# Attention turn of a transformer block: far scores ahead of the last near values, gated transposes ahead of the near scores, low half of the normalised rows behind the near maxima

## What is computed

```
OFFSETS = sorted(set(range(0, 33)) | {48, 64, 96, 128, 192, 256, 384})
q, k, v = split(x @ Wqkv + bqkv)
scores[o] = q . shift(k, o) * scale + pos_bias[o]        # -inf where the offset leads before row 0
out = sum_o softmax(scores)[o] * shift(v, o)
gate = sigmoid(x @ Wgate + bgate)
x = layernorm(x + (out * gate) @ Wout + bout)
logits = relu(x @ rw1 + rb1) @ rw2 + rb2                 # top 2 of 8 experts, capacity 1024
x = layernorm(x + experts(x))
```

## Time and profile before

| | |
|---|---|
| median of 3 runs | 1965.34 us |
| lowest, highest | 1961.47, 1973.05 us |
| span of the profiled execution, first to last instruction | 1999.0 us |
| the profiled execution's own time outside its span | not given; the span alone is 1.7% above the median |
| mean granted TensorE clock in the profiled execution | 0.797 of 2.4 GHz |
| PE, DVE, ACT, POOL busy | 1512.8, 989.1, 905.2, 708.5 us |

### The profile page before, as it was taken

One profiled execution on the slowest core, in us unless ns is written; L12 is line 12 of the kernel. 1 busy time (PEld: TensorE's weight loads), 2 busy tenths in 40 slices (PEclk: granted clock), 3 DMA queues, 4 the chain that ended last, 5 costly groups with the idle time before them and its releaser, 6 DMA issues. The chain is left out here.

```text
span 1999.0 us, 72320 instructions
## 1 busy us (share of the span) xinstructions
PE 1512.8 (76%) x31232; PEld 1001.5 (50%) x31232; DVE 989.1 (49%) x2117; ACT 905.2 (45%) x1544; POOL 708.5 (35%) x654
## 2 busy tenths in 40 slices
PE   2447777887778787877778787887875499999970
PEld 1235554555554554545555555555643266776660
DVE  5214455454554455455545455554645355555525
ACT  3123353444435353435445353545443366656626
POOL 6022233433334253333334252433323113323335
PEclk9566786868777797878778787878766699999995
DMA  4483453535243443525242433525210424443328
GB/s 120 91 227 93 88 105 81 112 90 111 76 102 79 88 104 79 116 77 112 64 105 73 88 92 68 110 72 110 57 47 14 140 75 91 101 105 87 72 30 339
DMA packets 220103, 194.55 MB, mean 97 GB/s; under 512 B 66847, under 2 KB 207151, under 8 KB 219648
## 3 DMA queue, kind: packets, MB, share of 16 engines
q1 hardware_dynamic: 204464, 175.11, 35.3%
q0 software_dynamic: 15360, 15.10, 4.7%
HBM read 98.07 MB, written 86.18 MB: 92 GB/s over the span
## 5 line engine op out<-in xcount | busy, mean ns | idle before, releaser
L396 POOL TENSOR_TENSOR p<-p 128x512 f16<-128x512 f32 x96 | 129.0, 1344 | 440.5 <-ACT p L796 427.4
L810 ACT COPY featT<-gp 128x1024 f16<-128x1024 f16 x96 | 93.4, 1032 | 321.3 <-PE gp L541 321.3
L396 DVE TENSOR_TENSOR p<-p 128x512 f16<-128x512 f32 x96 | 94.7, 987 | 284.7 <-ACT p L796 282.8
L548 PE MATMUL gp<-featT,wr 128*128 128x512 f16 x768 | 209.4, 432 | 22.8 <-DVE mT L959 13.8
L1107 POOL DMA_INDIRECT disp<-y,sidx x128 | 174.1, 1360 | 53.6 <-issue 38.0
L1364 POOL DMA_INDIRECT xln<-y,place x64 | 104.9, 1639 | 216.0 <-DVE y L1506 175.7
L1402 PE MATMUL up<-rowsT,w 128*128 128x512 f16 x768 | 171.3, 383 | 9.6 <-DVE w L1479 6.1
L1416 PE MATMUL dn<-w,h 128*128 128x256 f16 x1536 | 170.1, 273 | 0.0
L623 PE MATMUL o<-v_near,p 128*32 128x66 f16 x2048 | 132.3, 203 | 40.0 <-issue 28.4
L795 ACT ACTIVATE p<-st 128x512 f16<-128x512 f32 x192 | 116.7, 608 | 101.0 <-PE st L592 98.1
L1416 PEld LDWEIGHTS dn<-w,h 128*128 128x128 f16 x1536 | 149.7, 98 | 17.3
(11 more groups left out here) (176 smaller groups left out, 3127.0 us busy)
## 6 DMA issues: line engine op xcount, KB each, us to landing
qk_dram<-qk SPq DMA_DIRECT2D x64, 256.0 KB, 2.5
v_near<-vs SPq DMA_DIRECT2D x224, 66.0 KB
qs<-qk_dram SPq DMA_DIRECT2D x96, 128.0 KB, 4.4
ks<-qk_dram SPq DMA_DIRECT2D x96, 128.0 KB, 7.4
o_dram<-o_far SPq DMA_DIRECT2D x64, 136.0 KB, 5.7
o_back<-o_dram SPq DMA_DIRECT2D x16, 544.0 KB, 4.3
v_dram<-vs SPq DMA_DIRECT2D x16, 528.0 KB
v_far<-v_dram SPq DMA_DIRECT2D x64, 132.0 KB
```

The source lines that it names most:

```text
L396: engine.tensor_tensor(p16[:, b, 1, :], p32[:, b, :], p16[:, b, 0, :], ALU.subtract).then_inc(is_split, 1)
L548: last = nc.tensor.matmul(dst, lhs(a, c), rhs(b, c), start=(k == 0), stop=(k == len(todo) - 1))
L810: gp_done(nc.scalar.copy(featT[:, i, :, :].rearrange("f c t -> f (c t)"), bank[:, :].bitcast(F16)), n, stage, PART_OF_T[stage], i)
```

## The change

Three things are placed elsewhere; no instruction is added or taken away. The last near values (pair 5) move one slot later, behind the far scores of pair 0 and the x transposes, and half 0 of pair 0's exponentials goes one slot earlier, ahead of the copies of the x transposes. The gated transposes `outp t` move from slot 5 to slot 4 and the near scores of pair 2 from slot 4 to slot 5, so the transposes (and ScalarE's copies) come first. VectorE's L991 goes behind the near maxima.

```diff
-    3: [("rank", "l"), ("proj", "vg1")], 4: [], 5: [("outp", "t"), ("rank", "c")],
+    3: [("rank", "l"), ("proj", "vg1")], 4: [("outp", "t")], 5: [("rank", "c")],
@@ LATER
+         ("dve", "outp", "y"): 3,
@@
-SCORES_AT = [-1, 0, 4, 7, 10, 12]
-EXP_AT = [0, 1, 5, 8, 11, 13]
+SCORES_AT = [-1, 0, 5, 7, 10, 12]
+EXP_AT = [[-1, 1, 5, 8, 11, 13], [0, 1, 5, 8, 11, 13]]
 SPLIT_AT = [1, 2, 6, 9, 12, 14]
-VALUES_AT = [2, 4, 7, 10, 13, 15]
+VALUES_AT = [2, 4, 7, 10, 13, 16]
@@
-            def weights(n, k):
-                wait(act, pv_done, n.at(UNIT_PAIRS, k - 1))
-                for e in range(2):
-                    act.wait_ge(st_full[e], n.at(UNIT_PAIRS, k + 1))
...
+            def weights(n, k, e):
+                if e == 0:
+                    wait(act, pv_done, n.at(UNIT_PAIRS, k - 1))
+                act.wait_ge(st_full[e], n.at(UNIT_PAIRS, k + 1))
...
+            def tail(it, k):
                 for e in range(2):
...
+                    if pair_at(it, k, EXP_AT[e]):
+                        weights(*pair_at(it, k, EXP_AT[e]), e)
```

More of the change, by code:

```diff
@@ L788, in evacuate_far @@
                 last.then_inc(far_out, 1)
-            def weights(n, k):
-                wait(act, pv_done, n.at(UNIT_PAIRS, k - 1))
-                for e in range(2):
-                    act.wait_ge(st_full[e], n.at(UNIT_PAIRS, k + 1))
[L794 to L800, removed]
+            def weights(n, k, e):
+                if e == 0:
+                    wait(act, pv_done, n.at(UNIT_PAIRS, k - 1))
+                act.wait_ge(st_full[e], n.at(UNIT_PAIRS, k + 1))
+                bank, b = st[(2 * k + e) % ST_BANKS], 2 * (k % 2) + e
+                nc.scalar.activation(p16[:, b, 0, :], bank[:, :], ACT.Exp)
+                nc.scalar.activation(p32[:, b, :], bank[:, :], ACT.Exp).then_inc(exp_ready, 1)
+            def tail(it, k):
+                for e in range(2):
+                    if pair_at(it, k, EXP_AT[e]):
+                        weights(*pair_at(it, k, EXP_AT[e]), e)
                 if pair_at(it, k, EVAC_AT) and pair_at(it, k, EVAC_AT)[1] < FAR_PAIRS:
```

## The result

The changed kernel takes 1948.11 us (median; 1930.1 to 1952.74), the kernel before 1963.74 us beside it. The ratio is 0.9898, 95% interval 0.9855 to 0.9941: about 1% faster, where 3.1% was forecast and 1905 us; it lies inside the wide range, 1868 to 1950, by 2 us. The execution shown here took 1952.74 us, with a span of 1951.0.

The account below looks back on a forecast made before the run. TensorE's work and waits, with SP's transfer chain nearly as long, bound the turn. 4.4 us a turn over 14 turns, 61.6 us, scaled to 60.6, taken from 1965.3 gave 1905 us; own range 1880 to 1930, wide range 1868 to 1950.

Parts of the forecast that it names:

- The direction, the places and the order of waits: Pair 1's scores and the output projection stop waiting; near0 waits 3 to 5 us for the q/k stacks; faster, chance 0.89.
- The values end at t 5.3: Last near values, counted from the hidden layer's end: they end 3.0 us later; fetch follows at 23.4, near0 at 38.0.
- The q/k products at 5.4 us: The 24 q/k products behind pair 1's scores, without a standstill, run at the upper clock: 5.4 us instead of 7.14.
- near0's new wait: Ahead of near0: the output projection's gain becomes a wait of about 4 us for the q/k stacks.
- SP's issue time on the chain: SP's 16 `v_near` issues take 12.7 us and hold the q/k stores and the fetch; the skill's rule would give 1890.
- TensorE's work stays the same; the values now cover ScalarE.: Values behind far scores and x transposes: the 2.65 us standstill ahead of pair 1's scores goes; 4.4 us with q/k products.
- The turn's base: The turn followed takes 88.75 us, the mean 1.75 more, lost mostly at the same standstill; 0.5 of it was counted.
- The gated transposes: Moved ahead of pair 2's near scores: 3.32 us leave TensorE, not the turn; about 0.7 lower the residual sum's path.
- The low half: VectorE's L991, 1.23 us, behind the near maxima: the second maxima start right after the merge; its later place costs nothing.
- The sum: Whole turn: 4.45 us at the third maxima, 3.9 after near0's clock loss, 4.4 with 0.5 for longer turns.
- rival 2: Transfers take most of the gain: stacks land at t 41.0, 1.2 us a turn, 17 us, 1949; chance 0.14.
- the fetch-to-near0 term: From SP's fetch of the q/k stacks to near0: kept at 14.6 us; rival 2 has the fetch slow down by 3 us.

Follow-up runs that it names:

- the written-out kernel: The changed kernel with every engine's list written out, no loop on any engine: 1879.14 us, ratio 0.9614.
- splitting it: The changed kernel with all lists written out, second 8 of the 16 `v_near` transfers issued behind the fetch of the q/k stacks: 1906.43 us, ratio 0.9722.
- the second run of before: The kernel before, unchanged, profiled a second time: 1965.02 us, ratio 1.0004.

## Why the prediction was right, and where it was wrong

*The direction, the places and the order of waits*: right. Pair 1's scores and the output projection lost their waits, near0 gained one for the stacks, and the gated transposes do not wait for GpSimd's low half.

*"The values end at t 5.3", fetch 23.4, near0 38.0*: right as a chain, and shown by the written-out kernel (5.4, 23.5, 37.6); 14.1 us from fetch to near0 stand against the 14.6 kept. The q/k products at 5.4 us: 5.35. near0's new wait was put at 4 us and is 5.0 in the ten turns of the written-out kernel, since TensorE ends the output projection at 32.6 and not at 34. SP's issue time on the chain: right, as splitting it showed. The Trainium skill's rule in "DMA: Bandwidth & Descriptors", section "Issuing engines are not separate DMA queues", that the issuing time is usually small beside the transfer, does not hold for these 16 transfers in a row: SP's row says 12.12 us, 0.76 each, where one lands 2.1 us (median) after its issue begins.

*The step that failed: "TensorE's work stays the same; the values now cover ScalarE."* The step had no term for the branch. In five turns, TensorE's branch stood ahead of pair 1's scores and took 3.5 to 4.1 us. It began while the transposes still ran, and the standstill there of 2.9 to 3.5 us (2.89 at 813.28 in the earlier trace rows), which the prediction read as ScalarE's alone, covered nearly all of it: turns without a jump show 2.65. The change took that standstill away and put work that was ready, the values, right behind the branch. So the jump came to light: 4.3 to 5.2 us of standstill and 1.2 to 1.8 us more, and with it SP's `v_near`, the fetch and near0 all come later (12.4, 30.7, 44.8). The turns between jumps lose some as well: 0.6 to 1.35 us inside the transposes, and near0 at 40.3. With TensorE's list written out the kernel gives 1888.56 us. That leaves 59.6 us, 12 a jump, for TensorE's loop and what hangs on it, and when the jump alone was moved (1912.38), 36 us by the medians and 25 by the ratios came back. Of the 12, near0's delay explains 8.7 (6.6 behind a jump, 2.1 in the other turn, against 38.2); the other 3.5 arise behind near0. About 1.5 of them are gaps under "issue" there, which sum to 7.2 us over two turns and to 5.7 with TensorE's list written out; what makes them, and the rest, is open.

The cue was in the trace. Behind such a jump TensorE's timeline of the kernel before has a second gap, inside pair 1's scores; the scores' first line is in the earlier trace rows:

```profile
816.29 0.64 PE L572 MATMUL st<-qs,ks 49*32 49x32 f16 x44 [1.06 <-issue]
```

The turn that the prediction followed, from 724.53, has no such gap. The order listing quoted ahead of the prediction shows the branch between the transposes and the values, too, and the view of line 191 has the length of the jumps, which would have priced the missing term.

*The turn's base.* "Turns longer than the one followed lose their extra 1.75 us mostly at the same standstill" was wrong. Turns alternate, because every second one stands behind a jump (89.7 and 85.3 us in the second run of before), and the extra time does not end at pair 1's scores. The execution itself was 1.7% long, which scaling the gain by 0.983 does not mend: its turns do not scale alike.

*The gated transposes.* "The transfers, not this edit, fix near0": right for near0 (42.6 to 42.4 with this part alone), wrong as a worth of little. The part gives 17 us with the loop and 36 or more without.

*The low half*: 10 us by itself (1 less 0.9949), below the 1.2 us a turn that its row would give over 14 turns, and nothing that can be told beside the other two.

*The sum.* Predicted 4.4 us a turn. Without a loop it measures 5.1 (86.0 less 80.9). The gain was a little undersized, and the loss that was not foreseen took most of it.

*The rivals.* The time lies where rival 2 put it, 1949, but that is luck and not its mechanism: the fetch-to-near0 term did not grow (14.5 us, from 727.11 to 741.60). The stacks were late because the values were.

**Both kernels are beaten** by the changed kernel with TensorE's list written out (1888.56 us), by that with all lists written out (1879.14), and, keeping loops everywhere, by the moved border (1912.38).

## What to carry to other kernels

Mark where each engine's loop jumps before a step is priced, look up how long the branch takes in the view of the loop's line, since the timeline and the waits leave it out, and read the borders with a jump and those without one separately: a standstill that ends at the jump covers it, and taking the standstill away bares the jump. If a gain is to come from that place, first put the loop's border where the engine will wait anyway, or write that engine's list out, and measure either, for the jump need not keep its length in the new place. And when the trace names a releaser, look at whether the waiting work needs that very instance; the one it needs may have been done ten microseconds before.

## What the runs showed of the hardware that was not expected

- A backward jump of TensorE's loop took 3.5 to 5.5 us in slot 0 and 6.2 to 8.5 us in slot 6, the branch that left the loop 0.08 us, and the same loop's branches on the other four engines 0.04 to 0.07 us.
- With ready work behind it such a jump is a standstill of 4.3 to 5.2 us, then another of 1.2 to 1.8 us some matmuls later; in a program of 31232 matmuls, TensorE's loop with its five jumps was worth 59.6 us, with what they delayed.
- The timeline and the waits put all five of these standstills down to GpSimd's remainder; only the view of the loop's line names the branch.
- Lists written out are not free of such gaps: in the written-out changed kernel gaps of up to 2.4 us under "issue" appear in scattered places, such as this one in TensorE's timeline:

```profile
434.65 0.23 PE L539 MATMUL gp<-ident,x 128*128 128x128 f16 x1 [1.65 <-issue]
```

- The sixteen `v_near` transfers keep SP busy for 11.8 to 13.7 us in the kernel before and 10.8 to 12.6 in the changed one (over the ten turns), and halving their number moved the next stores by 3.5 us, not by 6.
